# The order of two VectorE instructions in a software pipeline: the second half of val and the product of val and gate

## The chip, the cores and the metric

The kernel runs on one core of a Trainium2 chip. The metric is the device time of one execution in microseconds (us), median of the runs; lower is better.

## The reference

The reference is a conditioned RMS norm, an up projection with a gated GELU, and a down projection with quantized activations and weights, with a residual. Shapes: x is 4 x 1024 x 512, cond 4 x 128, the up weight 4096 x 512 (val and gate, 2048 each), the down weight 512 x 2048.

```python
scale = cond @ norm_w.T + 1.0
ms = jnp.mean(x * x, axis=-1, keepdims=True)
h = x * (scale[:, None, :] * jax.lax.rsqrt(ms + EPS))
u = h @ up_w.T
val, gate = jnp.split(u, 2, axis=-1)
h = val * jax.nn.gelu(gate, approximate=False)
hq = act_quant(h)            # 127 / max|h| of each row, rounded
wq = weight_quant(down_w)    # 1 / mean|w|, rounded to -1, 0, 1
y = hq @ wq.T
return y + x
```

## The kernel before

The 4096 rows are cut into 8 blocks b of 512 (`NB` = 8, `TB` = 512, a half `HB` is 256), the 2048 hidden features into 16 tiles j of 128 (`J` = 16). One step n = 16 b + j makes one tile: 128 features of val and of gate for 512 rows. There are 128 steps, and each engine has its own program, written out by hand, in which the order of the instructions is fixed. Semaphores order the engines among each other; an engine that waits holds everything behind it in its program.

Each product of x and a weight is three fp16 matmuls (high by high, low by high, high by low parts; `product`, lines 571 to 585: 6 matmuls of 256 columns for two tiles of the contraction). In blocks 0 and 1 (steps 0 to 31) a tile is made directly, of 8 such products. From step 32 on (`in_seven`) it is made of 7 products with a Strassen scheme, whose partial results are combined between the products by ScalarE and VectorE. In step n TensorE does, in this order:

- `first_pair(n)`: two products into a bank of `ps_v` (3 banks); waits for `h_ready`, that is for `hidden(n-3)`, which frees the bank
- `third(n-1)`: one product; waits for `g_seeded`, that is for `seed_gate(n-1)` on VectorE
- `gates(n-1)`: two products into `ps_g` (2 banks); then the gate of tile n-1 is complete
- `second(n)`: one product; waits for ScalarE's two `copies(n)`
- `fourth(n-1)`: one product; waits for `v2_ready`, that is for `second_val(n-1)` on VectorE; then val of tile n-1 is complete
- behind it, in steps j = 0, 1, 2 and 15 of a block, a quarter of the down product of an earlier block (`down`, line 709, 16 matmuls of 512 columns)

ScalarE does in step n: `copies(n)` (lines 800, 803), `absolute(n-2)` (line 818, |h| of tile n-2 into g), `gelu(n-1)` (line 811), and then casts to the high parts of the next block's x (line 853), squares (line 837), and in block 2 `sum_high` (line 871).

VectorE does in step n, before the change:

- `hidden(n-2)` (line 1149): h = val x gate, 512 columns, waits for val and gate of tile n-2
- `second_val(n-1)` (line 1137): the second half of val of tile n-1 in PSUM, 256 columns; waits for `u3_ready`, that is for the end of `third(n-1)`
- `peak_of(n-2)` (line 1162, 1159 for j = 0): running maximum of |h|; waits for `absolute(n-2)`
- for j < 4 a residual add of the block before the last (line 1248)
- in steps j = 3 to 14 `scaled` (line 1227) for one tile of the last block, or two in steps 3, 6, 9 and 12 (`Q_COUNT = (2, 1, 1) * 4`)
- `seed_gate(n)` (line 1132): the second half of the gate of tile n in PSUM; waits for `second(n)`
- then `rounded` (line 1234) for the same tiles as `scaled`, `sum_low` (line 1058; in block 2 in steps j = 2, 3, 5, 6, 8), the dequantizing factors at j = 5 (line 1220), the norm of x for the next block at j = 1 (line 1098), differences and low parts of x (lines 1107 to 1127; in blocks 3 to 6 at j = 2, 4, 7, 10, 15), and at j = 11 of blocks 3, 4 and 5 the inverse root of the mean squares, twelve small instructions (`rsqrt`, lines 1071 to 1085)

Each of these is an instruction on 128 partitions. The SyncE queue issues all DMAs; weight low parts are loaded for each step (`load_lo`, waits for val of step n-1), and x, residual and output tiles at fixed steps.

Of the kernel before, what the change touches and what calls it, by code (L numbers as in the profile page):

```python
# [43 lines left out]
def bass_cond_norm_geglu_bitlinear(  # L44
# [27 lines left out]
    NJ = NB * J  # L72
# [20 lines left out]
    def in_seven(n):  # L93
        return n >= 2 * J

    def sevens(n):

        return n - 2 * J
# [37 lines left out]
    with ExitStack() as ctx:  # L136
# [176 lines left out]
        def by_vector(b):  # L313
            return V_FIRST <= b < NB - 1
# [14 lines left out]
        def rsqrt_at(c):  # L329
            return {1: 5, 2: 14, 3: J + 12, 4: 2 * J + 15}.get(c, (c - 2) * J + 11)  # L330
# [692 lines left out]
        def _(dve):  # L1023
            def power_of_two(slot, step, count, top, scale):

                a, p = peak_all[:, slot:slot + 1], p2[:, slot:slot + 1]
                dve.wait_ge(step, count)
                dve.tensor_scalar(p.bitcast(I32), a.bitcast(I32), EXPONENT, None, ALU.bitwise_and).then_inc(step, 1)
                dve.wait_ge(step, count + 1)
                return dve.tensor_scalar(scale.bitcast(I32), p.bitcast(I32), -1.0,  # L1030
                                         float((254 << 23) + int(math.log2(top)) * (1 << 23)), ALU.mult, ALU.add)

            def weight_scale(j):
                slot = j % 2
                dve.wait_ge(w_rows, j + 1)
                dve.tensor_reduce(peak_all[:, slot:slot + 1], ps_y[:, 1, slot * P:(slot + 1) * P], AX.X,
                                  ALU.max).then_inc(w_step, 1)
                if j >= 2:
                    dve.wait_ge(w_unscaled, j - 1)
                power_of_two(slot, w_step, 2 * j + 1, W_TOP, w_scale[:, j:j + 1]).then_inc(w_scaled, 1)  # L1040
# [94 lines left out]
            def second_val(n):  # L1135
                dve.wait_ge(u3_ready, sevens(n) + 1)
                dve.tensor_tensor(ps_v[:, n % NV, HB:TB], ps_v[:, n % NV, 0:HB], p5[:, sevens(n) % 2, :],  # L1137
                                  ALU.add).then_inc(v2_ready, 1)

            def hidden(n):  # L1140
                b, j = divmod(n, J)
                at = h_home(b, j) * TB
                dve.wait_ge(val_ready, n + 1)
                dve.wait_ge(g_ready, n + 1)
                if b >= 1 and j >= 2:
                    dve.wait_ge(q_ready, (b - 1) * J + Q_AT[j] + 1)
                if b >= 2 and j < 2:
                    dve.wait_ge(q_ready, (b - 2) * J + Q_AT[j] + 1)
                dve.scalar_tensor_tensor(out=h[:, at:at + TB], in0=ps_v[:, n % NV, :],  # L1149
                                         scalar=w_unscale[:, j:j + 1], in1=g[:, n % 3, :],  # L1150
                                         op0=ALU.mult, op1=ALU.mult).then_inc(h_ready, 1)
# [47 lines left out]
            def row_scales(b):  # L1199

                base = 3 * scaled_before(b)
                dve.wait_ge(max_rows, b + 1)
                dve.tensor_reduce(row_max, ps_m[:].rearrange("p (i n) -> p i n", i=TT), AX.X,
                                  ALU.max).then_inc(row_step, 1)
                dve.wait_ge(row_step, base + 1)
                dve.tensor_scalar(row_max, row_max, CLIP, None, ALU.max).then_inc(row_step, 1)
                dve.wait_ge(row_step, base + 2)
                dve.reciprocal(row_rec, row_max).then_inc(row_step, 1)
                dve.wait_ge(row_step, base + 3)
                dve.tensor_scalar(row_scale, row_rec, QMAX, None, ALU.mult).then_inc(scale_ready, 1)  # L1210
# [70 lines left out]
            for n in range(NJ + 2):  # L1281
                b, j = divmod(n, J)
                if 1 <= b < NB and j == 2 and not by_vector(b - 1):
                    row_scales(b - 1)
                if n == D_AT:
                    dve.wait_ge(d_summed, ND)
                    dve.tensor_reduce(d_sum[:], d_sums[:], AX.X, ALU.add).then_inc(d_sum_ready, 1)
                if b == 0 and 1 <= j < J - 1:
                    weight_scale(j + 1)
                if n >= 2:  # L1290
                    hidden(n - 2)
                if b == 0:
                    if j + 1 < J:
                        weight_low(j + 1)
                    if j == 7:
                        norm(1, 0)
                        norm(1, 1)
                    if j == 8:
                        norm(1, 2)
                        norm(1, 3)  # L1300
                    if j == 10:
                        low(1, XB11)
                        low(1, XB12)
                    if j == 11:
                        low(1, XB21)
                        low(1, XB22)
                if 1 <= n < NJ + 1 and in_seven(n - 1):
                    second_val(n - 1)
                if n >= 2:
                    peak_of(n - 2)  # L1310
                if b >= 2 and j < 4 and n < NJ:
                    residual(b - 2, j, ps_y[:, j % 2, :])
                k = j - Q_FIRST
                tiles = []
                if 1 <= b < NB and 0 <= k < len(Q_COUNT):
                    tiles = Q_ORDER[sum(Q_COUNT[:k]):sum(Q_COUNT[:k + 1])]
                for t in tiles:
                    scaled(b - 1, t)
                if n < NJ and in_seven(n):
                    seed_gate(n)  # L1320
                if 1 <= b < NB and j == 2 and by_vector(b - 1):
                    spread_peaks(b - 1)
                for t in tiles:
                    rounded(b - 1, t, q)
                for k in range(J):
                    if n == SUM_AT[k]:
                        sum_low(k)
                if n == D_AT + 1:
                    dve.wait_ge(d_rows, 1)

                    dve.tensor_copy(d_one[:], ps_y[:, 0, 0:1]).then_inc(d_step, 1)
                    dve.wait_ge(d_step, 1)
                    dve.tensor_scalar(ps_y[:, 0, 0:P], ps_y[:, 0, 0:P], d_one[:], None,
                                      ALU.subtract).then_inc(d_step, 1)
                    dve.wait_ge(d_step, 2)
                    dve.tensor_reduce(d_total[:], ps_y[:, 0, 0:P], AX.X, ALU.add).then_inc(d_step, 1)
                    dve.wait_ge(d_step, 3)
                    dve.scalar_tensor_tensor(out=d_total[:], in0=d_one[:], scalar=float(P), in1=d_total[:],
                                             op0=ALU.mult, op1=ALU.add).then_inc(d_step, 1)
                    dve.wait_ge(d_step, 4)  # L1340
                    dve.tensor_scalar(d_mean[:], d_total[:], 1.0 / (J * P * D), CLIP, ALU.mult,
                                      ALU.max).then_inc(d_step, 1)
                    dve.wait_ge(d_step, 5)
                    dve.reciprocal(d_scale[:], d_mean[:]).then_inc(d_scale_ready, 1)
                if 1 <= b < NB and j == 5:
                    row_dequant(b - 1)
                if 1 <= b < NB - 1:
                    if j == (0 if b == 1 else 1):
                        for kt in range(KT):
                            norm(b + 1, kt)  # L1350
                if 1 <= b < NB and j == 1 and by_vector(b - 1):
                    turn_peaks(b - 1)
                if 1 <= b < NB - 1:
                    if j == 2:
                        difference(b + 1, XT1)
                    if j == (2 if b < 3 else 4):
                        difference(b + 1, XT2)
                        low(b + 1, XB11)
                    if j == (2 if b < 3 else 7):
                        difference(b + 1, XT3)  # L1360
                        low(b + 1, XT1)
                    if j == (2 if b < 3 else 10):
                        difference(b + 1, XN4)
                    if j == 15:
                        for k in (XT2, XT3, XB21, XB22, XN4):
                            low(b + 1, k)
                for c in range(1, NB):
                    if n == rsqrt_at(c):
                        rsqrt(c)
# [56 lines left out]
```

## Time and profile before

| | |
|---|---|
| median of 3 runs | 751.35 us (749.39 to 752.73) |
| the profiled execution | 752.66 us |
| its span, first to last instruction | 750.8 us |
| mean granted TensorE clock | 0.998 |
| busy: TensorE, VectorE, ScalarE, GpSimd | 734.1, 561.5, 348.4, 99.4 us |
| span of steps 32 to 128 | about 200 to 722 us |

The times of instructions are those of the one profiled execution, in us from the start of its span. An instruction's row in the view in order of time has its start, its duration, the engine, the line, what it writes and reads, and, where the engine had been idle before it, how long and who ended that. Matmuls are pipelined: each is drawn about 0.27 us long though they start every 0.11 us, so their rows overlap.

### The profile page before, as it was taken

The page shows a single profiled execution, that of the slowest core. Times are in us where ns is not written, and L with a number is a line of the kernel's source. Part 1 is how long each engine was busy: PE and PEld are TensorE (multiplying, and loading weights), DVE is VectorE, ACT ScalarE, POOL GpSimd, SP SyncE. Part 2 cuts the span into 40 slices and gives each one's busy share as a digit, 9 for nine tenths or more (in the row PEclk, how much of TensorE's full clock was granted, in tenths as well). Part 3 has the DMA queues.
Part 4 walks back from the last instruction along what each step waited for, and adds up shares of the span by engine and source line. Part 5 has one row for each costly group of instructions (what it writes and reads, how often), then busy time and mean ns, then how long its engine had stood idle before and what let it go on. Part 6 is the DMA issues. An engine that isn't in the chain of part 4 may idle for free.

```text
span 750.8 us, 14329 instructions
## 1 busy us (share of the span) xinstructions
PE 734.1 (98%) x5480; PEld 536.2 (71%) x5480; DVE 561.5 (75%) x1126; ACT 348.4 (46%) x677; POOL 99.4 (13%) x137
## 2 busy tenths in 40 slices
PE   5999999999999999999999999999999999999998
PEld 4544444444577887888768887788878887688864
DVE  5467777887789776888768885898758886577757
ACT  4788856434254542455325543255424442143424
POOL 1211377783323000000000000000000000000000
PEclk9999999999999999999999999999999999999999
DMA  8887584656646545343543335343443333453202
GB/s 311 282 282 229 179 273 141 226 171 219 208 134 172 167 155 161 114 145 99 182 134 117 127 127 172 108 155 122 141 162 102 99 100 118 128 172 104 99 29 84
DMA packets 44788, 117.33 MB, mean 156 GB/s; under 512 B 5424, under 2 KB 5680, under 8 KB 43568
## 3 DMA queue, kind: packets, MB, share of 16 engines
q1 hardware_dynamic: 44720, 116.42, 47.8%
q8 instruction: 43, 0.70, 0.4%
q14 instruction: 25, 0.20, 0.1%
HBM read 99.62 MB, written 16.78 MB: 155 GB/s over the span
## 4 chain that ended last, share of the span: by engine, by line
PE 76%; DVE 12%; issue 5%; ACT 4%; DMA 1%; SPq 0%; DVEq 0%; POOL 0%; ACTq 0%
PE ps_v L582 13%; PE ps_v L584 13%; PE ps_v L583 13%; PE ps_y L709 12%; PE ps_g L584 5%; PE ps_g L582 5%; PE ps_g L583 5%; DVE h L1149 2%; DVE h_max L1162 2%; ACT g L818 2%; DVE h L1227 2%; DVE xs L1058 1%; PE ps_v L775 1%; DMA q<-in_up_t_dram 1%; PE ps_v L600 1%
## 5 line engine op out<-in xcount | busy, mean ns | idle before, releaser
L582 PE MATMUL ps_v<-x_hi,w_hi 128*128 128x256 f16 x968 | 264.2, 273 | 4.4 <-DVE ps_v L1137 1.5
L583 PE MATMUL ps_v<-x_lo,w_hi 128*128 128x256 f16 x968 | 264.1, 273 | 0.0
L584 PE MATMUL ps_v<-x_hi,w_lo 128*128 128x256 f16 x968 | 264.1, 273 | 0.0
L800 ACT COPY ps_g<-ps_v 128x256 f32<-128x256 f32 x96 | 34.3, 357 | 214.4 <-PE ps_v L584 214.4
L811 ACT ACTIVATE g<-ps_g,w_unscale 128x512 f32<-128x512 f32 x128 | 87.3, 682 | 66.9 <-PE ps_g L584 66.8
L1162 DVE TENSOR_TENSOR h_max<-g,h_max 128x512 f32<-128x512 f32 x120 | 85.6, 713 | 35.5 <-ACT g L818 28.2
L818 ACT ACTIVATE g<-h 128x512 f32<-128x512 f32 x128 | 81.3, 635 | 62.2 <-DVE h L1149 61.4
L1137 DVE TENSOR_TENSOR ps_v<-ps_v,p 128x256 f32<-128x256 f32 x96 | 41.3, 431 | 90.9 <-PE ps_v L584 90.8
L582 PEld LDWEIGHTS ps_v<-x_hi,w_hi 128*128 128x128 f16 x968 | 94.8, 98 | 20.3 <-DVE ps_g L1132 2.7
L584 PE MATMUL ps_g<-x_hi,w_lo 128*128 128x256 f16 x392 | 107.4, 274 | 0.0
L582 PE MATMUL ps_g<-x_hi,w_hi 128*128 128x256 f16 x392 | 107.3, 274 | 0.0
L583 PE MATMUL ps_g<-x_lo,w_hi 128*128 128x256 f16 x392 | 107.3, 274 | 0.0
L583 PEld LDWEIGHTS ps_v<-x_lo,w_hi 128*128 128x128 f16 x968 | 94.8, 98 | 13.4
L584 PEld LDWEIGHTS ps_v<-x_hi,w_lo 128*128 128x128 f16 x968 | 94.8, 98 | 11.1
L709 PE MATMUL ps_y<-dw,q 128*128 128x512 bf16 x448 | 101.3, 379 | 0.0
L1149 DVE SCALAR_TENSOR_TENSOR h<-ps_v,w_unscale,g 128x512 f32<-128x512 f32 x128 | 95.5, 746 | 2.4 <-PE ps_v L584 2.2
L1227 DVE TENSOR_TENSOR h<-h,ps_m 128x512 f32<-128x512 f32 x128 | 84.1, 681 | 1.8 <-PE ps_m L698 1.8
L709 PEld LDWEIGHTS ps_y<-dw,q 128*128 128x128 bf16 x448 | 43.8, 98 | 47.1
L1132 DVE TENSOR_TENSOR ps_g<-ps_v,p 128x256 f32<-128x256 f32 x96 | 41.2, 430 | 10.0 <-PE ps_v L584 5.9
L1234 DVE TENSOR_SCALAR q<-h 128x512 bf16<-128x512 f32 x112 | 47.4, 444 | 0.3
L600 PE MATMUL ps_v<-x_hi,w_hi 128*128 128x512 f16 x124 | 47.0, 379 | 0.6 <-DVE h L1149 0.6
L600 PE MATMUL ps_g<-x_hi,w_hi 128*128 128x512 f16 x124 | 47.0, 379 | 0.0
(139 smaller groups left out, 925.3 us busy)
## 6 DMA issues: line engine op xcount, KB each, us to landing
w_lo<-w_lo_dram SPq DMA_DIRECT2D x96, 448.0 KB, 3.3
q<-in_up_t_dram SPq DMA_DIRECT2D x16, 512.0 KB, 4.9
xt<-in_x_cols_dram SPq DMA_DIRECT2D x8, 1024.0 KB, 5.2
res<-in_x_rows_dram SPq DMA_DIRECT2D x26, 256.0 KB, 3.6
out_dram<-res SPq DMA_DIRECT2D x26, 256.0 KB, 2.7
sums<-in_up_t_dram SPq DMA_DIRECT2D x12, 512.0 KB, 4.6
xs<-in_x_rows_dram SPq DMA_DIRECT2D x22, 256.0 KB, 3.7
w_lo_dram<-w_lo SPq DMA_DIRECT2D x16, 256.0 KB, 4.3
```

Of the source, the lines that this page charges most:

```text
L582: pe.matmul(to, w_hi[:, wh:wh + P], hi, start=start and kt == 0, stop=False, skip_group_check=True)
L583: pe.matmul(to, w_hi[:, wh:wh + P], lo, start=False, stop=False, skip_group_check=True)
L584: last = pe.matmul(to, w_lo[:, wl:wl + P], hi, start=False, stop=(kt == 1), skip_group_check=True)
L600: pe.matmul(bank, w_hi[:, wh:wh + P], hi, start=start and kt == 0, stop=False)
L709: last = pe.matmul(ps_y[:, i % 2, :], q[:, j * TB + i * P:j * TB + (i + 1) * P], dw[:, j * D:(j + 1) * D], start=(j == 0), stop=(j == J - 1))
L811: act.activation(g[:, n % 3, :], ps_g[:, n % NG, :], ACT.Gelu, scale=w_unscale[:, n % J:n % J + 1]).then_inc(g_ready, 1)
L818: act.activation(g[:, n % 3, :], h[:, at:at + TB], ACT.Abs).then_inc(h_abs_ready, 1)
L1137: dve.tensor_tensor(ps_v[:, n % NV, HB:TB], ps_v[:, n % NV, 0:HB], p5[:, sevens(n) % 2, :], ALU.add).then_inc(v2_ready, 1)
L1149: dve.scalar_tensor_tensor(out=h[:, at:at + TB], in0=ps_v[:, n % NV, :], scalar=w_unscale[:, j:j + 1], in1=g[:, n % 3, :], op0=ALU.mult, o ...
L1162: dve.tensor_tensor(h_max[:], g[:, n % 3, :], h_max[:], ALU.max).then_inc(h_max_ready, 1)
L1227: dve.tensor_tensor(h[:, at:at + TB], h[:, at:at + TB], ps_m[:], ALU.mult).then_inc(scaled_ready, 1)
L1234: dve.tensor_scalar(to[:, j * TB:(j + 1) * TB], h[:, at:at + TB], ROUND, ROUND, ALU.add, ALU.subtract).then_inc(q_ready, 1)
```

## The change

On VectorE, in each step n from 33 to 128, `second_val(n-1)` is issued in front of `hidden(n-2)`, and no longer behind it. Nothing else is changed; steps below 33 have no `second_val`.

```diff
                 if b == 0 and 1 <= j < J - 1:
                     weight_scale(j + 1)
+                if 1 <= n < NJ + 1 and in_seven(n - 1):
+                    second_val(n - 1)
                 if n >= 2:
                     hidden(n - 2)
                 if b == 0:
...
                     if j == 11:
                         low(1, XB21)
                         low(1, XB22)
-                if 1 <= n < NJ + 1 and in_seven(n - 1):
-                    second_val(n - 1)
                 if n >= 2:
                     peak_of(n - 2)
                 if b >= 2 and j < 4 and n < NJ:
```

## Rows read from the trace of the kernel before

**Rows 1.** The page: busy time by engine, and TensorE's clock in 40 slices
```profile
PE 734.1 (98%) x5480; PEld 536.2 (71%) x5480; DVE 561.5 (75%) x1126; ACT 348.4 (46%) x677; POOL 99.4 (13%) x137
...
PEclk9999999999999999999999999999999999999999
```

**Rows 2.** TensorE's waits, 200 to 722 us: total us, times, longest
```profile
PE ps_v L582 <- DVE ps_v L1137: 1.5, 1, 1.5
PE ps_v L582 <- DVE ps_g L1132: 1.3, 5, 0.5
```

**Rows 3.** Busy time of each engine in two stretches
```profile
core 0: us, PE busy (x) PEld busy (x) DVE busy (x) ACT busy (x) POOL busy (x), PEclk, DMA share, GB/s
200.00:722.00 522.00, 519.10 (x4386) 428.43 (x4385) 396.84 (x815) 216.99 (x457) 13.27 (x16) 1.00 0.43 134
...
236.00:248.00 12.00, 10.28 (x94) 8.64 (x92) 10.97 (x18) 5.03 (x11) 3.88 (x4) 1.00 0.47 130
```

**Rows 4.** VectorE in order of time, block 3, steps 10 to 12
```profile
340.80 0.43 DVE L1137 TENSOR_TENSOR ps_v<-ps_v,p 128x256 f32<-128x256 f32 x1 [0.48 <-PE ps_v L584]
...
345.39 0.43 DVE L1137 TENSOR_TENSOR ps_v<-ps_v,p 128x256 f32<-128x256 f32 x1 [0.60 <-PE ps_v L584]
...
348.02 0.16 DVE L1071 TENSOR_SCALAR ms<-sumsq 128x4 f32<-128x4 f32 x1
...
350.32 0.75 DVE L1149 SCALAR_TENSOR_TENSOR h<-ps_v,w_unscale,g 128x512 f32<-128x512 f32 x1
...
351.77 0.69 DVE L1162 TENSOR_TENSOR h_max<-g,h_max 128x512 f32<-128x512 f32 x1 [0.36 <-ACT g L818]
...
353.57 0.43 DVE L1132 TENSOR_TENSOR ps_g<-ps_v,p 128x256 f32<-128x256 f32 x1
```

**Rows 5.** TensorE in order of time: the first matmuls of third and of gates
```profile
344.53 0.27 PE L582 MATMUL ps_v<-x_hi,w_hi 128*128 128x256 f16 x1
...
345.19 0.27 PE L582 MATMUL ps_g<-x_hi,w_hi 128*128 128x256 f16 x1
```

**Rows 6.** VectorE in order of time, block 3, steps j = 3 to 5
```profile
308.71 0.43 DVE L1137 TENSOR_TENSOR ps_v<-ps_v,p 128x256 f32<-128x256 f32 x1 [1.37 <-PE ps_v L584]
...
309.87 0.75 DVE L1248 SCALAR_TENSOR_TENSOR res<-ps_y,dequant,res 128x512 f32<-128x512 f32 x1
310.53 1.28 DVE L1227 TENSOR_TENSOR h<-h,ps_m 128x512 f32<-128x512 f32 x2
311.72 0.43 DVE L1132 TENSOR_TENSOR ps_g<-ps_v,p 128x256 f32<-128x256 f32 x1
312.06 0.76 DVE L1234 TENSOR_SCALAR q<-h 128x512 bf16<-128x512 f32 x2
...
316.04 0.69 DVE L1113 TENSOR_TENSOR tb<-xt,ta 128x512 f32<-128x512 f32 x1
...
317.24 0.75 DVE L1149 SCALAR_TENSOR_TENSOR h<-ps_v,w_unscale,g 128x512 f32<-128x512 f32 x1
...
320.56 0.97 DVE L1220 TENSOR_SCALAR dequant<-row_peak,d_mean 32x4 f32<-32x4 f32 x4
```

**Rows 7.** ScalarE and TensorE in order of time, around the stall at 354
```profile
351.11 0.63 ACT L818 ACTIVATE g<-h 128x512 f32<-128x512 f32 x1 [1.15 <-DVE h L1149]
...
354.06 0.28 PE L582 MATMUL ps_v<-x_hi,w_hi 128*128 128x256 f16 x1 [0.20 <-DVE ps_g L1132]
```

**Rows 8.** VectorE in order of time, block 2, step j = 6
```profile
236.68 1.77 DVE L1234 TENSOR_SCALAR q<-h 128x512 bf16<-128x512 f32 x2
238.37 1.74 DVE L1058 SCALAR_TENSOR_TENSOR xs<-sums,w_scale,w_hi 128x1024 f16<-128x1024 f32 x1
```

## The prediction, made before the changed kernel was run

> **What bounds the kernel now.** The first view to read is the page: TensorE is busy for 98% of the span and its granted clock stands at nine tenths or more in all forty slices [rows 1]. So a change on VectorE can win only what TensorE still waits for, and can lose whatever it makes TensorE wait for. The second view is TensorE's own list of waits in the part where `second_val` exists, steps 32 to 128, which are 200 to 722 us of the span: VectorE's second half of val was waited for once, 1.5 us, and VectorE's `seed_gate` five times, 1.3 us together [rows 2]. The third view gives the whole of it: in those 522 us TensorE was idle for 522.00 - 519.10 = 2.9 us [rows 3]. That is the most that can be won, 0.4% of the kernel. What is left is to see how far VectorE's results come ahead of the time at which TensorE wants them. That is read from the order of time.
>
> **TensorE's beat.** In a step without down products TensorE issues `first_pair(n)`, `third(n-1)`, `gates(n-1)`, `second(n)`, `fourth(n-1)`: 42 matmuls, and from one `second_val` to the next such a step takes 345.39 - 340.80 = 4.59 us [rows 4]. I call the start of the first matmul of `third` T. The six matmuls of `third` stand between 344.53 and the first one into ps_g at 345.19 [rows 5], and `second_val` starts at 345.39 [rows 4], so `second_val` can start at T + 0.86. `fourth` begins 24 matmuls after T, 24 x 4.59/42 = 2.62 us, so `second_val` (0.43 long) may be 2.62 - 0.86 - 0.43 = 1.3 us late before TensorE feels it. What TensorE wants next is `seed_gate(n)`, at the next T, 4.59 us later.
>
> **The change part by part.** It removes and adds no instruction and no DMA: 96 times VectorE's 256-wide add is put in front of the 512-wide multiplication. No wait is new; two change places. (1) `hidden(n-2)`, which could start before `third(n-1)` was done, now stands behind `second_val(n-1)`, which waits for it. (2) `peak_of(n-2)` waits for ScalarE's `absolute(n-2)`, which waits for `hidden(n-2)`; the add used to fill a part of that wait. Now nothing stands between `hidden` and `peak_of`. Behind `peak_of` in VectorE's queue are, in order, the residual add (steps j = 0 to 3), k multiplications `scaled` (k = 2 at j = 3, 6, 9, 12, else 1 for j = 4 to 14, none at j = 15, 0, 1, 2) and `seed_gate(n)`, for which `third(n)` waits.
>
> What each costs, from rows. An instruction's successor on VectorE starts before its end: behind the add of 0.43 the next starts 312.06 - 311.72 = 0.34 later; the residual add gives 310.53 - 309.87 = 0.66, two `scaled` give 311.72 - 310.53 = 1.19, so 0.60 each [rows 6], and I take 0.60 for `peak_of`, which is of the same shape and duration as one `scaled`. From `hidden`'s start to `peak_of`'s: 351.77 - 350.32 = 1.45 [rows 4], ScalarE's 0.63 us being in the middle of it [rows 7]. From the end of a late `seed_gate` (353.57 + 0.43 [rows 4]) to TensorE's first matmul (354.06 [rows 7]): 0.06.
>
> Before, the chain from T to the next T was, in its longest case, j = 3: `second_val` at 308.71, `seed_gate` over at 311.72 + 0.43 = 312.15 [rows 6], so 0.86 + 3.44 + 0.06 = 4.36 us, just under 4.59: hidden by TensorE's own work. Now it is 0.86 + 0.34 (`second_val`) + 1.45 (`hidden`, absolute) + 0.60 (`peak_of`) + 0.60 k + 0.66 (only j = 3) + 0.43 + 0.06 = 3.74 + 0.60 k (+ 0.66). With k = 1 that is 4.34, still hidden; with k = 2 it is 4.94, so **TensorE waits 0.35**; at j = 3 it is 5.60 and TensorE waits 1.01. Any lateness L of `second_val` is added to it. L comes from what VectorE does behind `seed_gate`: it is free 2.73 + 0.93 k + E after a `second_val` (2.73 = 0.34 + 1.45 + 0.60 + 0.34; 0.60 + 0.33 for each `scaled` and its rounding), and E is 317.24 - 316.04 = 1.20 for a difference with its low part at j = 4 and 7, 0.97 for dequant at j = 5 [rows 6], 350.32 - 348.02 = 2.30 for the inverse root at j = 11 of blocks 3, 4 and 5 [rows 4].
>
> Block by block, L carried on. Blocks 3, 4, 5: j = 3 waits 1.01; j = 4 leaves L = 2.73 + 0.93 + 1.20 - 4.59 = 0.27; j = 5 waits 0.02 and leaves 0.32; j = 6 waits 3.74 + 0.32 + 1.20 - 4.59 = 0.67; j = 8 waits 0.02; j = 9 waits 0.35; j = 11 leaves L = 3.66 + 2.30 - 4.59 = 1.37; j = 12 waits 3.74 + 1.37 + 1.20 - 4.59 = 1.72. Sum 3.79. Of this, 0.36 was there before: at 354.06 TensorE had been idle 0.20 [rows 7], and a stall is 0.16 longer than the idle shown, because a matmul is drawn 0.27 long where they follow each other in 0.11. So 3.43 x 3 = 10.3 us. Block 6 has no inverse root: 1.01 + 0.02 + 0.67 + 0.02 + 0.35 + 0.35 = 2.4. Block 7 has no x work: 1.01 + 0.42 + 0.35 + 0.35 = 2.1. In steps j = 15, 0, 1, 2 a down product of 3.45 us gives each step 8.04 us, and 2.73 + 0.66 + E (at most some 4 us) fits in.
>
> Block 2 is the one where VectorE is already behind, with `sum_low` in five steps, and where some of its instructions run longer than elsewhere: two roundings took 1.77 and the `sum_low` after it 1.74 [rows 8]. I run the same sum through it with those rows as they stand. It comes out at +0.8 at j = 3, +0.25 at j = 4, +0.4 at j = 5, +1.1 at j = 6, +0.3 at j = 7, +0.7 at j = 9, +0.35 at j = 12: 3.9 us; in it is a relief, since `second_val` no longer stands behind `hidden` (0.66) where TensorE waited 1.5 for it. The bounds are 2 (no stretching) and 6 (the stretches fall on the chain each time).
>
> **Sum**: 10.3 + 2.4 + 2.1 + 3.9 = **+18.7 us**. The profiled execution took 752.66 us for a span of 750.8; it becomes 771.4. It lay 1.3 us above the median of the runs shown, so the median goes from 751.35 to **770.0**. The tail costs nothing: the last `peak_of` moves by some 0.4 us and is hidden by the down product before the transposes that need it. DMA is not touched: loads wait for val and for x parts, and those shift with TensorE.
>
> Where VectorE hands on to itself, the rows say that the successor starts 0.09 before the end (0.34 behind an instruction of 0.43 [rows 6]). The Trainium skill, "Advanced Engine Details and Errata", section "The Read-Write Bubble", says that memory latency is exposed as a bubble between VectorE's instructions. The trace does not agree for these shapes: the starts overlap.
>
> **Rivals.**
> (A) As above, stalls at `seed_gate`: +18.7, chance 0.82.
> (B) The other side: the seeds are never late, and only waits go. For this the chain from `second_val` to `seed_gate` would have to be 0.35 shorter in the k = 2 steps and 1.01 shorter at j = 3; then at most the 2.9 us of idle time [rows 3] are won, 748.5. Against it: the chain is made of real dependences and rows; for it: only that VectorE has idle time in total. It decides at a chain of 4.59. Chance 0.05.
> (C) The chain is shorter by some 0.35 (`hidden` or absolute handed on faster than the loaded rows show): then stalls remain at j = 3 (0.66 x 6), at j = 6 (0.3 x 5), at j = 12 (1.0 x 3) and in block 2 (2.5): +11, 762. Chance 0.06.
> (D) Handing on costs more in the new order, a full duration instead of 0.09 less. Then k = 2 gives 5.30, the steps with k = 1 reach 4.61, L is carried from step to step, and blocks 3 to 5 lose some 8 each, block 6 six, block 7 four, block 2 seven: +40, 791. No row shows it. Chance 0.04. A full bubble between instructions, as that page has it, would make it so.
> (E) The new stalls cost TensorE its clock. The longest would be 1.72 us; in 236 to 248 us a wait of 1.5 stood and the granted clock was 1.00, the 2.4 GHz level [rows 3]. Were one step behind each of the three long stalls run at half of that, each would cost another 4.59: +33, 784. Chance 0.03. The Trainium skill, "TensorE: Matmul & The Clock Gate", section "A second HAM failure mode: psum-queue depth-cycling", tells of frequent small pauses that let the clock swing. The trace does not show it with pauses of this size.
>
> **Range.** The bounds of (A): 24 seeds wait, each 0.1 to 0.2 us off gives -2 to +5, block 2 gives -2 to +2, run to run 1 to 2. With (C) inside, 758 to 782 us leaves (B), (D) and (E) outside, 0.12. What this kernel's measurement can tell from no change is about 0.5%, 3.8 us. Slower by more: (A), (C), (D), (E), 0.95. Within: (B), most of it, 0.04. Faster by more: 0.01, as 2.9 us is less than 3.8.
>
> **What would show it.** TensorE's waits for `seed_gate` rise from 5 to at least 24, about 15 us of idle time, in steps j = 3, 6, 9, 12 of each block; its wait for `second_val` is gone. VectorE's busy time stays; its idle time before `peak_of` grows to about 0.7 us in nearly all of the 96 steps, and is put down to absolute. In an unloaded step `peak_of` starts 1.8 us behind `second_val` where it was 0.55. The steps with k = 1 stay at 4.59 between two `second_val`; if they do not, L is larger than I say and (D) is the way. If the stalls are there but the three at j = 12 are not near 1.7, the term for the inverse root is wrong. I would be wrong in sign if VectorE could reach `seed_gate` without `peak_of`; in the order as written it cannot.

## The result, and the profile after

The changed kernel takes 769.98 us (median of 4 runs, 769.38 to 770.36) against 750.88 for the kernel before in the same comparison. The ratio is 1.0256, with a 95% interval of 1.0237 to 1.0276: 2.6% slower. The forecast was 770.0, with stalls at `seed_gate` as in (A). The profiled execution has a span of 768.6 us, 17.8 above the 750.8 of before; the sum had said 18.7.

The page of the changed kernel, its line of busy time and TensorE's clock in 40 slices, answers to [rows 1]:

```profile
PE 738.2 (96%) x5480; PEld 533.4 (69%) x5480; DVE 555.9 (72%) x1126; ACT 344.5 (45%) x677; POOL 98.7 (13%) x137
...
PEclk9999999999999999999999999999999999999999
```

The counts are the same, so no engine has more to do, and TensorE's share falls because the span is longer. Its busy time is 4.1 us larger, which is the way in which matmuls are drawn: the last one before a stall is not overlapped by the next, and 0.16 us for each of 26 waits make 4.2. VectorE's busy time is 5.6 us smaller; what the change added is waiting. TensorE's waits in steps 32 to 128, which now last to 741 us, answer to [rows 2]:

```profile
PE ps_v L582 <- DVE ps_g L1132: 15.6, 26, 1.4
PE ps_v L582 <- DVE ps_v L1137: 0.6, 1, 0.6
```

The wait for `second_val`, in front of which the change put nothing any more, fell from 1.5 to 0.6 us. The waits for `seed_gate`, which the change does not name at all, rose from 1.3 us in 5 to 15.6 us in 26. Busy time by stretch answers to [rows 3]:

```profile
core 0: us, PE busy (x) PEld busy (x) DVE busy (x) ACT busy (x) POOL busy (x), PEclk, DMA share, GB/s
358.00:361.00 3.00, 1.64 (x16) 1.22 (x15) 2.85 (x6) 1.34 (x4) 0.00 (x0) 1.00 0.52 154
200.00:741.00 541.00, 524.64 (x4392) 426.23 (x4390) 391.01 (x817) 213.41 (x457) 13.48 (x16) 1.00 0.41 129
```

TensorE is idle for 541.00 - 524.64 = 16.4 us where it was 2.9: 13.5 us more, and with the 4.1 us of longer drawn time that is 17.6. The first stretch, 3 us long, holds one of the longest stalls, and the granted clock stays at 1.00, the 2.4 GHz level. Who waits longest over the whole execution (total, times, longest) shows where the time was put in:

```profile
ACT g L818 <- DVE h L1149: 189.1, 113, 6.9
ACT ps_g L800 <- PE ps_v L584: 175.1, 86, 5.8
DVE h_max L1162 <- ACT g L818: 80.7, 115, 0.8
DVE ps_v L1137 <- PE ps_v L584: 80.3, 74, 5.0
```

The largest row, ScalarE's absolute waiting for `hidden`, is no cost in itself: ScalarE has time. The third row is the one that matters: `peak_of` waits for absolute 115 times, 0.7 us on average. In the steps from 32 on, this row was the first one before and is the second one now:

```profile
DVE h_max L1162 <- ACT g L818: 9.6, 28, 0.4
DVE h_max L1162 <- ACT g L818: 62.6, 90, 0.7
```

VectorE in order of time, block 3, steps j = 3 to 6, answers to [rows 6]:

```profile
311.62 0.43 DVE L1137 TENSOR_TENSOR ps_v<-ps_v,p 128x256 f32<-128x256 f32 x1 [1.22 <-PE ps_v L584]
311.96 0.74 DVE L1149 SCALAR_TENSOR_TENSOR h<-ps_v,w_unscale,g 128x512 f32<-128x512 f32 x1
313.40 0.69 DVE L1162 TENSOR_TENSOR h_max<-g,h_max 128x512 f32<-128x512 f32 x1 [0.69 <-ACT g L818]
314.01 0.74 DVE L1248 SCALAR_TENSOR_TENSOR res<-ps_y,dequant,res 128x512 f32<-128x512 f32 x1
314.67 1.27 DVE L1227 TENSOR_TENSOR h<-h,ps_m 128x512 f32<-128x512 f32 x2
315.87 0.42 DVE L1132 TENSOR_TENSOR ps_g<-ps_v,p 128x256 f32<-128x256 f32 x1
...
317.21 0.43 DVE L1137 TENSOR_TENSOR ps_v<-ps_v,p 128x256 f32<-128x256 f32 x1 [0.26 <-PE ps_v L584]
...
322.07 0.42 DVE L1137 TENSOR_TENSOR ps_v<-ps_v,p 128x256 f32<-128x256 f32 x1
...
326.60 0.41 DVE L1137 TENSOR_TENSOR ps_v<-ps_v,p 128x256 f32<-128x256 f32 x1
...
331.64 0.43 DVE L1137 TENSOR_TENSOR ps_v<-ps_v,p 128x256 f32<-128x256 f32 x1 [0.26 <-PE ps_v L584]
```

Read the first six rows as a chain: add, `hidden` 0.34 later, `peak_of` 1.44 after that with 0.69 of it idle, residual, two `scaled`, seed. The seed begins 315.87 - 311.62 = 4.25 us behind the add; before it was 311.72 - 308.71 = 3.01 [rows 6]. TensorE, at the end of that seed (this row answers to the stall in [rows 7]):

```profile
316.35 0.28 PE L582 MATMUL ps_v<-x_hi,w_hi 128*128 128x256 f16 x1 [0.83 <-DVE ps_g L1132]
```

0.83 idle and 0.16 for the overlap in which matmuls are drawn: 0.99 us, where the forecast for j = 3 was 1.01. The end of the block, the starts of steps j = 11 to 13, answers to [rows 4]:

```profile
350.47 0.43 DVE L1137 TENSOR_TENSOR ps_v<-ps_v,p 128x256 f32<-128x256 f32 x1 [0.25 <-PE ps_v L584]
...
354.12 0.16 DVE L1071 TENSOR_SCALAR ms<-sumsq 128x4 f32<-128x4 f32 x1
...
356.38 0.42 DVE L1137 TENSOR_TENSOR ps_v<-ps_v,p 128x256 f32<-128x256 f32 x1
...
361.30 0.43 DVE L1137 TENSOR_TENSOR ps_v<-ps_v,p 128x256 f32<-128x256 f32 x1 [0.26 <-PE ps_v L584]
```

The stall at the end of that step is the one behind the inverse root:

```profile
360.44 0.28 PE L582 MATMUL ps_v<-x_hi,w_hi 128*128 128x256 f16 x1 [1.36 <-DVE ps_g L1132]
```

1.36 idle and 0.16 are 1.52 us. The two steps from 350.47 to 361.30 take 10.83 us, 1.65 more than two beats of 4.59, where the forecast was 1.72. Of the 0.13 that the stall does not hold, 0.04 stand in front of `fourth`, which waited for the late `second_val`, and 0.07 in front of the next `first_pair`, at 357.60; there `hidden` (over at 357.45) may have been late, which would be all that place (1) cost in this step.

Where the time went, by block, is read from the starts of `second_val` at the same step of each block (in step j = 1; for block 2 the first one, the end of block 7 is the last one at 738.0, before at 720.3). For before, blocks 3, 4, 6 and 7, and below them for after, blocks 3 to 7:

```profile
292.63 0.43 DVE L1137 TENSOR_TENSOR ps_v<-ps_v,p 128x256 f32<-128x256 f32 x1 [5.10 <-PE ps_v L584]
380.17 0.43 DVE L1137 TENSOR_TENSOR ps_v<-ps_v,p 128x256 f32<-128x256 f32 x1 [4.67 <-PE ps_v L584]
...
555.26 0.43 DVE L1137 TENSOR_TENSOR ps_v<-ps_v,p 128x256 f32<-128x256 f32 x1 [4.67 <-PE ps_v L584]
642.43 0.43 DVE L1137 TENSOR_TENSOR ps_v<-ps_v,p 128x256 f32<-128x256 f32 x1 [4.67 <-PE ps_v L584]
```

```profile
295.55 0.43 DVE L1137 TENSOR_TENSOR ps_v<-ps_v,p 128x256 f32<-128x256 f32 x1 [5.00 <-PE ps_v L584]
386.55 0.43 DVE L1137 TENSOR_TENSOR ps_v<-ps_v,p 128x256 f32<-128x256 f32 x1 [4.57 <-PE ps_v L584]
477.42 0.43 DVE L1137 TENSOR_TENSOR ps_v<-ps_v,p 128x256 f32<-128x256 f32 x1 [4.57 <-PE ps_v L584]
568.29 0.43 DVE L1137 TENSOR_TENSOR ps_v<-ps_v,p 128x256 f32<-128x256 f32 x1 [4.57 <-PE ps_v L584]
657.84 0.43 DVE L1137 TENSOR_TENSOR ps_v<-ps_v,p 128x256 f32<-128x256 f32 x1 [4.57 <-PE ps_v L584]
```

| block | before, us | after, us | more | forecast |
|---|---|---|---|---|
| 2 | 292.63 - 201.09 = 91.54 | 295.55 - 201.08 = 94.47 | 2.93 | 3.9 |
| 3 | 380.17 - 292.63 = 87.54 | 91.00 | 3.46 | 3.43 |
| 4 | 87.54 | 90.87 | 3.33 | 3.43 |
| 5 | 87.55 | 90.87 | 3.32 | 3.43 |
| 6 | 642.43 - 555.26 = 87.17 | 89.55 | 2.38 | 2.4 |
| 7 | 720.3 - 642.43 = 77.9 | 738.0 - 657.84 = 80.2 | 2.3 | 2.1 |
| sum | 519.2 | 536.9 | 17.7 | 18.7 |

The first add stands at 201.1 in both, and behind the last one there are 30.5 us before and 30.6 after. So all of the difference is in this table. In the kernels below I call the time from the first to the last `second_val` the stretch: 519.2 before, 536.9 after. It is the cleaner measure, though it rests on one profiled execution of each kernel: the first `second_val` stood between 198.0 and 201.6 us in the profiled executions, though the code ahead of it was the same in all but e6 and e7.

### The profile page after: what moved, and what is told of

It is laid out like the page before. It is cut to its first block, busy times and chain, and to the rows that moved or that the text cites. A ratio compares the mean times of both kernels' runs of the same rounds, so it can differ in the third digit from the quotient of the medians.

```text
span 768.6 us, 14329 instructions
## 1 busy us (share of the span) xinstructions
PE 738.2 (96%) x5480; PEld 533.4 (69%) x5480; DVE 555.9 (72%) x1126; ACT 344.5 (45%) x677; POOL 98.7 (13%) x137
## 4 chain that ended last, share of the span: by engine, by line
PE 58%; DVE 23%; issue 9%; ACT 7%; DMA 1%; SPq 0%; DVEq 0%; POOL 0%; ACTq 0%
PE ps_y L709 12%; PE ps_v L582 9%; PE ps_v L584 9%; PE ps_v L583 9%; DVE h L1149 5%; DVE h L1227 5%; ACT g L818 4%; PE ps_g L582 3%; PE ps_g L584 3%; PE ps_g L583 3%; DVE h_max L1162 2%; DVE ps_g L1132 2%; DVE xs L1058 1%; PE ps_v L775 1%; PE ps_v L600 1%
## 5 line engine op out<-in xcount | busy, mean ns | idle before, releaser
L582 PE MATMUL ps_v<-x_hi,w_hi 128*128 128x256 f16 x968 | 264.5, 273 | 17.6 <-DVE ps_g L1132 15.6
L811 ACT ACTIVATE g<-ps_g,w_unscale 128x512 f32<-128x512 f32 x128 | 85.7, 670 | 0.0
L601 PE MATMUL ps_g<-x_lo,w_hi 128*128 128x512 f16 x124 | 47.0, 379 | 0.0
L602 PE MATMUL ps_g<-x_hi,w_lo 128*128 128x512 f16 x124 | 47.0, 379 | 0.0
```

Source lines behind the costliest of these rows:

```text
L582: pe.matmul(to, w_hi[:, wh:wh + P], hi, start=start and kt == 0, stop=False, skip_group_check=True)
L601: pe.matmul(bank, w_hi[:, wh:wh + P], lo, start=False, stop=False)
L602: last = pe.matmul(bank, w_lo[:, wl:wl + P], hi, start=False, stop=not start and kt == 1)
L811: act.activation(g[:, n % 3, :], ps_g[:, n % NG, :], ACT.Gelu, scale=w_unscale[:, n % J:n % J + 1]).then_inc(g_ready, 1)
```

## The experiments

The forecast gave one cause: absolute and `peak_of` now stand in the chain from one `third` to the next, without cover, in front of `seed_gate`. Rival 1 is that `hidden`, which frees the val bank, is late behind the add. Rival 2 is that VectorE has become the bound by its work and idle time in total, wherever it stands. Eight kernels were made; two of them were run a second time. Each ratio is to the kernel before, timed in the same comparison (e1 to e4 in one, e5 to e8 in a second, e9 and e10 in a third, the changed kernel in its own), so small differences are read from the ratios and the stretches, and not from the medians alone.

| kernel | median, us | ratio to before, 95% | stretch, us | expected, us |
|---|---|---|---|---|
| the changed one | 769.98 | 1.0256 (1.0237 to 1.0276) | 536.9 | 770.0 |
| e1 peak_of behind the seed | 747.41 | 0.996 (0.9944 to 0.9977) | 516.1 | 748 to 751 |
| e2 scaled fills the wait | 751.51 | 1.001 (0.9999 to 1.0022) | 519.8 | 752.5 |
| e3 scaled behind the seed | 756.19 | 1.0073 (1.0054 to 1.0092) | 524.3 | 755.5 |
| e4 residual behind the seed | 767.60 | 1.0221 (1.0202 to 1.024) | 535.1 | 767.5 |
| e5 no absolute | 751.65 | 1.0017 (1.0004 to 1.0031) | 519.8 | 754 |
| e6 two root rounds | 766.57 | 1.0209 (1.0185 to 1.0234) | 535.1 | 768.2 |
| e7 counts 1, 1, 2 | 770.16 | 1.0263 (1.0237 to 1.0288) | 539.0 | 772 |
| e8 old order, peak_of behind the seed | 748.94 | 0.9979 (0.9965 to 0.9993) | 517.2 | 749 to 751 |
| e9, e1 again | 747.05 | 0.9944 (0.9925 to 0.9963) | 515.7 | 747.4 |
| e10, e8 again | 749.78 | 0.9979 (0.9966 to 0.9992) | 517.9 | 749 |

**e1: take `peak_of` out of the chain.**

```diff
-                if n >= 2:
+                if n >= 2 and not in_seven(n):
                     peak_of(n - 2)
...
                 if n < NJ and in_seven(n):
                     seed_gate(n)
+                if n >= 2 and in_seven(n):
+                    peak_of(n - 2)
```

> Changed order, but from step 32 on peak_of(n-2) is issued behind seed_gate(n), no longer in front of it. Theory (TensorE waits for seed_gate because absolute and peak_of stand in front of it): the chain from T to T becomes 0.86 + 0.34 + 0.66 + 0.60 k (+ 0.66) + 0.43 + 0.06 = 2.35 + 0.60 k, at most 4.2 us, under the beat of 4.59; the waits for seed_gate go from 26 to nearly none, and the time falls by some 18 us or more below the changed kernel: 748 to 751. Rival 1 (the cost is that hidden, and with it the release of the val bank, stands behind the add): hidden is where it was, so the time stays at 770. Rival 2 (VectorE has become the bound by its own work and idle time): the same instructions, and a wait of 0.7 us taken out of each step, so it falls too, but in the steps with much x work first, to some 760.

It took 747.4, and TensorE's idle time in the stretch is gone:

```profile
200.00:741.00 541.00, 540.62 (x4494) 439.35 (x4491) 407.56 (x852) 222.84 (x471) 14.00 (x16) 1.00 0.40 129
```

```profile
PE ps_v L582 <- DVE ps_v L1137: 0.3, 1, 0.3
```

Both views show 0.3 to 0.4 us left, and no wait for the seed. (The window is that of the changed kernel; here the stretch ends at 714.1.) `hidden` stands behind the add as in the changed kernel, so rival 1 is out. Rival 2 named 760 for this kernel; it is out for it too.

**e2: fill the wait.**

```diff
-                if n >= 2:
+                if n >= 2 and not in_seven(n):
                     peak_of(n - 2)
-                if b >= 2 and j < 4 and n < NJ:
-                    residual(b - 2, j, ps_y[:, j % 2, :])
...
                 for t in tiles:
                     scaled(b - 1, t)
+                if n >= 2 and in_seven(n):
+                    peak_of(n - 2)
+                if b >= 2 and j < 4 and n < NJ:
+                    residual(b - 2, j, ps_y[:, j % 2, :])
                 if n < NJ and in_seven(n):
                     seed_gate(n)
```

> Changed order, but from step 32 on the k multiplications scaled are issued between hidden and peak_of, where VectorE waits 0.7 us for ScalarE's absolute; the residual add stands behind peak_of. Theory: the chain is 0.86 + 0.34 + max(1.45, 0.66 + 0.60 k) + 0.60 + 0.43 + 0.06: 3.74 with k = 1, 4.15 with k = 2, 4.81 at j = 3 (a wait of 0.22), and at j = 12 behind the inverse root 4.15 + 0.77 (0.33). The loss over before is some 1.5 us: 752.5. Rival 1 (hidden late): 770. A rival in which only the amount of work on VectorE counts: the work is the same, only the idle time before peak_of goes; the gain over the changed kernel would be under 10 us.

Step j = 3 of block 3:

```profile
308.85 0.43 DVE L1137 TENSOR_TENSOR ps_v<-ps_v,p 128x256 f32<-128x256 f32 x1 [1.22 <-PE ps_v L584]
309.19 0.74 DVE L1149 SCALAR_TENSOR_TENSOR h<-ps_v,w_unscale,g 128x512 f32<-128x512 f32 x1
309.85 1.28 DVE L1227 TENSOR_TENSOR h<-h,ps_m 128x512 f32<-128x512 f32 x2
311.04 0.69 DVE L1162 TENSOR_TENSOR h_max<-g,h_max 128x512 f32<-128x512 f32 x1
311.64 0.75 DVE L1248 SCALAR_TENSOR_TENSOR res<-ps_y,dequant,res 128x512 f32<-128x512 f32 x1
312.30 0.43 DVE L1132 TENSOR_TENSOR ps_g<-ps_v,p 128x256 f32<-128x256 f32 x1
...
313.65 0.43 DVE L1137 TENSOR_TENSOR ps_v<-ps_v,p 128x256 f32<-128x256 f32 x1 [0.26 <-PE ps_v L584]
```

The two `scaled` lie in the time in which absolute runs, and `peak_of` follows with no idle time. The step is 313.65 - 308.85 = 4.80 us, 0.21 over the beat (forecast 0.22). Same instructions, same place of `hidden`, `peak_of` still in front of the seed: 17 of the 17.7 us of the stretch are back. So it is the idle time in front of `peak_of` that costs, together with what follows it ahead of the seed.

**e3: `scaled` behind the seed.**

```diff
-                for t in tiles:
-                    scaled(b - 1, t)
                 if n < NJ and in_seven(n):
                     seed_gate(n)
+                for t in tiles:
+                    scaled(b - 1, t)
```

> Changed order, but scaled is issued behind seed_gate instead of in front of it; peak_of stays in front. Theory: the chain no longer holds k: 3.74 in each step, 4.40 at j = 3, both under 4.59; but VectorE's total per step is as large as before, so the lateness of second_val grows (L up to 1.1 at j = 7) and is what is left: waits of 0.27 at j = 8, 0.1 at j = 5 and 6, 0.52 at j = 12, about 0.9 in each of blocks 3 to 5, 0.4 in block 6, none in block 7, some 2.5 in block 2. Time about 755.5. Rival 1 (hidden late): 770. Rival 2 (VectorE is the bound): 770 too, since nothing of its work or idle time is taken away.

It took 756.2, the stretch 5.1 us over before. The idle time in front of `peak_of` is all there (63.3 us in the stretch), and the loss is 5.1 us in place of 17.7, under a third. TensorE waits 1.8 us for the seed in 10 short waits and 2.3 us for `second_val`. So the place of work in front of the seed is most of the cost. What is left goes with lateness that VectorE carries from step to step, as the expectation had it; rival 2, the total on VectorE, can have this share and no more.

**e4: the residual behind the seed.**

```diff
-                if b >= 2 and j < 4 and n < NJ:
-                    residual(b - 2, j, ps_y[:, j % 2, :])
...
                     seed_gate(n)
+                if b >= 2 and j < 4 and n < NJ:
+                    residual(b - 2, j, ps_y[:, j % 2, :])
```

> Changed order, but the residual add is issued behind seed_gate. Theory: the wait at j = 3 falls by 0.66 (1.01 to 0.35), but VectorE is then late by 0.31 and gives 0.06 back at j = 4 and 0.25 at j = 5; net 0.4 in each of blocks 3 to 6, 0.6 in block 7, 0.3 in block 2: 2.4 us less than the changed kernel, 767.5. A sum without carried lateness would say 6 x 0.66 = 4.0 less: 766.

767.6. The stretch is 1.8 us shorter, less than the 4.0 of a sum without carried lateness and nearer the 2.4 with it. What is taken out of the chain at j = 3 comes back in part one and two steps later, because VectorE has the same work. In block 4 the gaps between TensorE's matmuls show it: the stall at j = 3 is 0.34 in place of 0.99, and j = 4 and 5 now lose 0.05 and 0.26 (expected 0.06 and 0.25). The list of waits shows nothing at j = 4, since a gap under 0.16 us is covered by the way in which matmuls are drawn. The 0.6 us that are missing are mostly in block 2, which was 0.1 us longer and not 0.3 shorter.

**e5: absolute left out.**

```diff
-                if n >= 2:
+                if n >= 2 and not in_seven(n - 2):
                     absolute(n - 2)
...
-                dve.wait_ge(h_abs_ready, n + 1)
+                at = h_home(b, j) * TB
+                src = h[:, at:at + TB] if in_seven(n) else g[:, n % 3, :]
+                if in_seven(n):
+                    dve.wait_ge(h_ready, n + 1)
+                else:
+                    dve.wait_ge(h_abs_ready, n + 1)
...
-                    dve.tensor_tensor(h_max[:], g[:, n % 3, :], h_max[:], ALU.max).then_inc(h_max_ready, 1)
+                    dve.tensor_tensor(h_max[:], src, h_max[:], ALU.max).then_inc(h_max_ready, 1)
```

This kernel leaves out the magnitude: from tile 32 on its maximum is that of h and not of |h|. It also takes that work off ScalarE; e1 and e2 leave it there.

> Changed order, but from tile 32 on ScalarE's absolute is left out, and peak_of takes the running maximum of h itself (not of its magnitude) straight from hidden's output. Theory: ScalarE's 0.63 us go out of the chain; hidden is followed by peak_of after about 0.8 instead of 1.45, and the chain is about 3.10 + 0.60 k. Waits are left at j = 3 (0.37) and at j = 12 of blocks 3 to 5 (0.44), and some in block 2: about 3 us over before, 754. Rival 1 (hidden late): 770, since the order is the same.

751.65, below the 754 expected. In block 3, step j = 3, `peak_of` is line 1167 here:

```profile
306.35 0.74 DVE L1149 SCALAR_TENSOR_TENSOR h<-ps_v,w_unscale,g 128x512 f32<-128x512 f32 x1
307.13 0.69 DVE L1167 TENSOR_TENSOR h_max<-h,h_max 128x512 f32<-128x512 f32 x1
...
309.59 0.42 DVE L1132 TENSOR_TENSOR ps_g<-ps_v,p 128x256 f32<-128x256 f32 x1
```

0.78 from `hidden` to `peak_of` in place of 1.44: ScalarE's part of the chain is 0.66. In block 4 the waits left at j = 3 and j = 12 are 0.34 and 0.33 (expected 0.37 and 0.44). Block 2 took 90.4 us, 1.1 less than before, where I had some more in mind; that is most of the difference.

**e6: a shorter inverse root.**

```diff
-        RS_STEPS = 11
+        RS_STEPS = 8
...
-                for k in range(3):
+                for k in range(2):
```

(with the last round's condition moved from 2 to 1.)

> Changed order, but the inverse root makes two refinement rounds instead of three (a less exact root): three small instructions, 0.60 us, less in each. Theory: L at j = 11 of blocks 3 to 5 falls from 1.37 to 0.77, and the wait at j = 12 by the same: 3 x 0.60 = 1.8 less than the changed kernel, 768.2, and block by block between second_val at j = 12 and 13 of blocks 3, 4, 5 0.6 less. If lateness of second_val were covered by its own room of 1.3 us before fourth, nothing would change there.

The stretch is 1.8 us shorter, as expected, and in blocks 3, 4 and 5 the time between `second_val` at j = 11 and at j = 12 is 5.32 or 5.33 us in place of 5.91 (the expectation named the step behind it, whose 4.92 stayed as it was). The median of 766.6 is lower than expected. In the profiled execution the part ahead of the stretch was 2.5 us shorter too (its first `second_val` stood at 198.6 in place of 201.1), which would account for it; four of the shortened roots stand there, but kernels that left that part alone spread as far. So lateness of `second_val` is passed on to the seed in full; its own room of 1.3 us before `fourth` does not cover it.

**e7: other counts.**

```diff
-    Q_COUNT = (2, 1, 1) * 4
+    Q_COUNT = (1, 1, 2) * 4
```

> Changed order, but the tiles are scaled in counts 1, 1, 2 instead of 2, 1, 1: k = 2 at j = 5, 8, 11, 14. Theory: j = 3 waits 0.41 instead of 1.01, but now k = 2 follows the x work: 0.62 at j = 5, 0.37 at j = 6, 0.62 at j = 8, 0.35 at j = 11, 1.70 at j = 12, 0.35 at j = 14; 0.6 more in each of blocks 3 to 5, 0.3 more in block 6, as much in block 7: about 2 us more than the changed kernel, 772. Whoever counts only k = 2 steps and the residual would say 4 us less.

The stretch is 2.1 us longer, as expected; the median, 770.2, can't be told from the changed kernel's. (The edit also moves `scaled` in block 1, ahead of the stretch.) Taking the double step away from the residual did not help, since it then fell behind the x work and in front of the inverse root.

**e8, e9, e10: what the change is worth when the seed is out of reach.** e8 is the kernel before with the edit of e1.

> The order of before (hidden, then second_val), with peak_of behind seed_gate as in e1. It shows what the change is worth once the seed is out of reach. Theory: nothing but the stalls of before is left, and some of those in block 2 go, since the wait for absolute is gone; 749 to 751. Against e1 it keeps second_val behind hidden, 0.66 later when VectorE is behind: e1 should be faster by the stalls behind the inverse root (0.36 x 3) and a part of block 2, 0.5 to 1.5 us, little more than can be measured.

> The kernel of e1 (changed order, peak_of behind seed_gate) once more, with more rounds and beside e10 on the same chip: 747.4, 0.4% to 0.5% under the kernel before.

> The kernel of e8 (order of before, peak_of behind seed_gate) once more: 749, 0.2% to 0.3% under the kernel before, and 1 to 2 us above e9. If the change has a value of its own once the seed is out of reach, this gap is it.

With `peak_of` behind the seed, the new order (e9) took 747.05 and the old order (e10) 749.78. The intervals of their ratios to before, 0.9925 to 0.9963 and 0.9966 to 0.9992, do not touch. In the stretch it is 2.1 us: 0.35 us in each of blocks 3 to 5, which hold the inverse root, and 1.1 us in block 2. The first pair, e1 and e8, is 1.5 us apart in the median, with intervals that overlap, and 1.1 us in the stretch: the same 0.35 in each of blocks 3 to 5, but only 0.1 in block 2. There one and the same kernel took 89.6 us in e8 and 90.3 in e10. So the change itself is worth 1 to 3 us once the instruction that it exposes has been moved; of this, 1.05 us stand in the same place in both pairs, and the part in block 2 is not shown. The kernel of e1 is faster than the changed one and the one before, than the latter by 0.4 and 0.6% in its two runs.

## Why the prediction was right, by its steps

**The bound on a gain.** 2.9 us of idle time were to be had at most. e1, which has all of it, is 3.4 to 4.2 us below the kernel before in the median and 3.1 to 3.5 in the stretch. Idle time understates each of the six stalls by 0.16, as said in the working, so the bound should have been put at 2.9 + 1.0 = 3.9 us.

**Two places.** Place (1), `hidden` behind the add, costs next to nothing by itself: e1 has it and is faster than before, e2 has it and is 0.6 us over in the stretch. Place (2), the uncovered wait for absolute, is the cause: e5 takes ScalarE out of it, e2 covers it, e1 moves it away, and each gives back 17 us or more.

**The chain.** The term 3.74 + 0.60 k (+ 0.66) held to a few hundredths: 0.99 measured at j = 3 for 1.01. The forecast of the time in block 4 from the `second_val` of step j to the next one, worked out from T and L, against what stood there:

| j | 3 | 4 | 5 | 6 | 7 | 8 | 9 | 10 | 11 | 12 |
|---|---|---|---|---|---|---|---|---|---|---|
| forecast | 5.60 | 4.86 | 4.66 | 4.94 | 4.86 | 4.34 | 4.94 | 4.59 | 5.96 | 4.94 |
| measured | 5.59 | 4.85 | 4.53 | 5.04 | 4.86 | 4.32 | 4.93 | 4.59 | 5.91 | 4.92 |

**Carried lateness.** e4, e6 and e7 are the tests: a term taken out, one made smaller, the same terms in another order. In the stretch each came out within 0.6 us. One sentence of the text was wrong as it stood: that the steps with k = 1 stay at 4.59 between two `second_val`. T stays on its beat, or nearly so; `second_val` moves by the change of L, so 4.85 and 4.53 are seen. The largest misses of the table, at j = 5 and 6, undo each other: `second_val` came 0.11 earlier, and `hidden` 0.45 behind it and not 0.34. One small slip in the sum: L behind j = 5 comes to 0.30 and not 0.32, since the wait of 0.02 makes that step longer.

**Block 2** is the term that was mis-sized: 3.9 said, 2.9 measured. I had run the sum "with those rows as they stand", that is with the lengthened instructions of before in their places. They do not all keep them. Before, step j = 5 had

```profile
228.94 1.24 DVE L1162 TENSOR_TENSOR h_max<-g,h_max 128x512 f32<-128x512 f32 x1 [0.33 <-ACT g L818]
...
231.04 0.82 DVE L1234 TENSOR_SCALAR q<-h 128x512 bf16<-128x512 f32 x1
```

In the changed kernel both were at their usual length, and the two roundings of step j = 6 took 0.24 less:

```profile
231.46 0.69 DVE L1162 TENSOR_TENSOR h_max<-g,h_max 128x512 f32<-128x512 f32 x1 [0.69 <-ACT g L818]
...
233.00 0.42 DVE L1234 TENSOR_SCALAR q<-h 128x512 bf16<-128x512 f32 x1
...
238.57 1.53 DVE L1234 TENSOR_SCALAR q<-h 128x512 bf16<-128x512 f32 x2
240.01 1.74 DVE L1058 SCALAR_TENSOR_TENSOR xs<-sums,w_scale,w_hi 128x1024 f16<-128x1024 f32 x1
```

The last two rows answer to [rows 8]. The steps fit: the forecast had +0.4 at j = 5 and +1.1 at j = 6, and what came was no stall at j = 5 and 0.72 at j = 6, where there had been 0.33. How much of the 1.0 us is chance is open: the two executions of one kernel differ in block 2 by 0.3 us (e1, e9) and 0.7 us (e8, e10). What lengthens these instructions was not tried. GpSimd's adds of `sum_weights` run at the same time, one of them 1.59 long beside the last of these rows, but that is only a coincidence in time so far.

**The total is in part luck.** The forecast came within 0.1 us of the median because two errors had opposite signs. The profiled execution was to take 771.4 us and took 770.36, 1.0 less, which is block 2. And I took 1.3 us off for the place of the profiled execution above its median, where it lay 0.4 above. Between the medians the loss is 19.1 us, between the profiled spans 17.8; the sum, 18.7, lies between them.

**The rivals.** (B) and (C) fell: no seed chain was shorter than the rows by the 0.35 that they need. (D) fell: in 89 of the 96 steps `hidden` starts 0.33 to 0.35 behind the `second_val` of 0.43, as the rows said; in the other seven it is 0.45 to 0.47. (E) fell: 26 stalls of up to 1.4 us idle, and the mean granted clock is 0.997, against 0.998. **The signs named**: at least 24 waits for the seed, about 15 us of idle time (26 and 15.6; the two beyond the 24 are at j = 4 and 7 of block 2); `peak_of` 1.8 us behind the add (313.40 - 311.62 = 1.78); the wait for `second_val` gone (0.6 left, once, in block 2); a stall near 1.7 at j = 12 (1.65).

**A reading that goes too far.** From rows whose starts lie before the end of the row in front, the prediction concludes that no gap is exposed between VectorE's instructions. The rows do not show that. From start to start, 256 columns take 0.34 us and 512 columns 0.60: 256 columns more cost 0.26, so, as an estimate, about 0.08 us of each instruction do not grow with its columns. The sum is not touched by this, as it goes by starts.

## What to carry to other kernels

An instruction that waits for another engine is cheap as long as something useful stands between the instruction that feeds that engine and itself; before moving a short piece of work out of such a gap, ask what fills it then, and who is queued behind the waiting instruction. Compare the whole chain from one product to the next with the beat of the bounding engine, step by step and with the lateness carried on: here the steps with k = 1 had 0.25 us of room (4.34 against 4.59) and the steps with double work had none. When an order exposes a wait, try to move the waiting instruction itself behind the one that the bounding engine wants; that made the same change a gain of 1 to 3 us in place of a loss of 18 to 19.

## What was not expected of the hardware

The part ahead of the stretch differed by up to 3.6 us between profiled executions of kernels with the same code there, e6 and e7 left out (first `second_val` at 198.0 to 201.6); the first `hidden` already spread over 2.4 us, from 27.1 to 29.5. What causes it is open. For kernels that differ by less than 0.5%, a stretch between two fixed instructions tells more than the total.
